# Cross-attention with head size 32: probabilities turned by VectorE's 32x32 squares and transfers instead of TensorE, value sums normalised after the product

## The chip, the cores and the metric

The kernel runs on one core of one Trainium2 chip. The metric is the device time of one execution in microseconds (us), median of several runs. Only the first attention of the network, about 230 us of some 2250 us, is touched.

## The reference

The network is a stack of two models over the same activations, x of 8 batches x 112 rows x 512, and the same context of 8 batches x 375 keys x 512. The changed part is the attention of the first model (16 heads of size 32):

```python
B, LQ, _ = hidden_states.shape          # 8, 112, 512
q = (x @ q_w + q_b).reshape(B, LQ, H, HD).transpose(0, 2, 1, 3)       # H = 16, HD = 32
k = (encoder_hidden_states @ k_w + k_b).reshape(B, LK, H, HD)...      # LK = 375
v = (encoder_hidden_states @ v_w + v_b).reshape(B, LK, H, HD)...
scores = jnp.einsum('bhqd,bhkd->bhqk', q, k) * scale
scores = jnp.where(mask, scores, mask_value)
attn = jax.nn.softmax(scores, axis=-1)
out = jnp.einsum('bhqk,bhkd->bhqd', attn, v)
out = out.transpose(0, 2, 1, 3).reshape(B, LQ, D) @ cproj_w + cproj_b
hidden = out + residual                 # then layer norm, fc, gelu, proj, residual
```

The second model follows: two cross-attentions with 16 heads of size 128, and an MLP. It is not changed.

## The kernel before

All is float32; a product of two float32 operands is three fp32r products over high and low halves (`product`, L1892 to L1894). Each engine runs its own hand-ordered program; semaphores join them. The changed stage is `attend_first`, which exists once for each engine. The stage before it writes the queries to memory, the stage behind it (`project` with layer 0) is the output projection and the next layer norm.

The stage runs over 8 batches, and in each over 4 tiles `t` of four heads, so over 32 tiles; a head of a tile is a unit `j`. In the iteration of tile T:

- TensorE (PE) makes the scores of the four heads of tile T+1 (`score_quad`, L2012: three rounds of four 32-row products into four banks `ps_s0`, of which one is the bank `ps_t[1]` and one `ps_o[1]`). Then for each j it turns the probabilities of head j of tile T with three transposes into one bank (`turn`, L2025), and fills in a quarter of other work (`fill`: half a key tile for tile T+2 by `key`, or part of the values of the next batch by `value`). At the end `weighted` (L2037) multiplies the turned probabilities by the values: 12 plain float32 products into `ps_o0`.
- ScalarE (ACT) evicts each turned head to `prob_t` in SBUF (`turned`, L1106), makes the exponentials of tile T+1 with their row sums (`exp`, L1110), the high half of the keys (L1100), the value tiles (L1086) and the high half of the output (`output_hi`, L1116).
- VectorE (DVE) makes the masked maxima of tile T+1 from the score banks (`masked_maximum`, L1576), and behind each exponential the reciprocal of the row sum (L1550) and the normalisation of the 112x375 probabilities (L1553), both in `normalize`; further the low half of the keys (L1559), of the output (`output_lo`, L1586) and of the queries (`split_q`, L1546), and once in a batch the high half of a context (`context_hi`, L1530).
- GpSimd (POOL) makes the low half of a context once in a batch (L916).
- SyncE (SP) issues all DMAs, on one queue. In this stage these are, once in a batch, the queries of the next batch (L687), a copy of the context from memory to memory for later (L636) and the context of the batch after the next (L632); further, in the first and the last batch, four transfers of weights (L612).

The second model's attention already has what the change brings to the first, once in a batch (not in a tile): VectorE turns 32x32 squares into an image `blocks` of 128 x 1536 (L1682), SP stores it (768 KB, `store_blocks`, L746), waits until it has landed, and loads it back with bands and squares exchanged, in four DMAs of 192 KB into 32 partitions each (`load_turned`, L756):

```python
src = turned_scr[place.parity].rearrange("(i a) (s f) -> s a i f", i=BANDS, s=4)
for s in range(4):
    rows = slice(SQUARE * s, SQUARE * (s + 1))
    dst = pt[place.parity][1][rows, :].bitcast(F32).rearrange("a (i f) -> a i f", i=BANDS)
    sp.dma_start(dst, src[s]).then_inc(turned_in[place.parity], 16)
```

Of the kernel before, what the change touches and what calls it, by code (L numbers as in the profile page):

```python
# [9 lines left out]
ALU = mybir.AluOpType  # L10
# [173 lines left out]

def wait(eng, sem, value):

    if isinstance(value, int) and value <= 0:
        return
    eng.wait_ge(sem, value)


def build(nc, x_in, ctx_in, kd_in_all, mask_in, blocks_a, blocks_b, vec_a, vec_b, value_rows, value_bias_rows, row_bias, eye, out):
# [7 lines left out]
    with ExitStack() as ctx:  # L200
# [15 lines left out]
        with ExitStack() as first_use:  # L216
# [5 lines left out]
            prob_2 = passing("prob2", [P, LK])  # L222
        sums_hi = sb("sums_hi", [P, DT, 4 * HALF], F32R)
        with ExitStack() as first_use:
            act_t_lo = passing("act_t_lo", [P, DT, ROWS], F32R)
            ctx_raw = [passing(f"ctx_raw{i}", [P, 3 * D]) for i in range(2)]
            prob_3 = passing("prob3", [P, LK])
        sums_lo = sb("sums_lo", [P, DT, 4 * HALF], F32R)
        act_t, sums = [act_t_hi, act_t_lo], [sums_hi, sums_lo]
        with ExitStack() as first_use:  # L230
            shared = passing("shared", [P, SUB0 * 3 * LQ])
            mask_u8 = passing("mask_u8", [LQ, NB * LK], U8)
            key_add = passing("key_add", [LQ, LK])
        extra = sb("extra", [P, 4 * NT * P + HALF])
# [15 lines left out]
        prob_t = [shared[:, 3 * LQ * i:3 * LQ * (i + 1)] for i in range(SUB0)]  # L250
# [5 lines left out]
        blocks = sb("blocks", [P, BLOCKS * P])  # L256
        extra_p = sb("extra_p", [P, 2 * NT])
# [20 lines left out]
        ps_s0, ps_t0, ps_o0 = [*ps_s, ps_t[1], ps_o[1]], ps_t[0], ps_o[0]  # L278
# [33 lines left out]
        t_mm, t_ev, av_mm = sem("t_mm"), sem("t_ev"), sem("av_mm")  # L312
# [83 lines left out]
        def turn_bank(place, t, j):  # L396

            return ps_v if place.final and t == 0 and j % 2 else ps_t0

# [4 lines left out]
        def key_evicted(place, t, j):  # L404

            if place.final:
                return place.key(t + 2) if j == 2 and t < 2 else None
            kind, part = fill(place, t, j)
            return part[0:2] if kind == KEY and part[2][1] == DT else None
# [193 lines left out]
        def _(sp):  # L603
# [277 lines left out]
        def _(pool):  # L881
# [44 lines left out]
            def attend_first():  # L926
                def one_batch(place):
                    for t in range(NT):
                        if t == 2 and place.after(2):
                            context_lo(place.after(2))  # L930

# [62 lines left out]
        def _(act):  # L994
# [98 lines left out]

            def attend_first():
# [8 lines left out]
                def turned(place, t, j):  # L1103
                    act.wait_ge(t_mm, place.unit + SUB0 * t + j + 1)
                    wait(act, av_mm, place.tile + t)
                    act.activation(prob_t[j][:], turn_bank(place, t, j)[:, 0:3 * LQ], ACT.Identity).then_inc(t_ev, 1)  # L1106

# [6 lines left out]
                def output_hi(place, t):  # L1114
                    act.wait_ge(av_mm, place.tile + t + 1)
                    act.activation(act_t[0][:, t, ds(place.b * LQ, LQ)], ps_o0[:, 0:LQ], ACT.Identity,  # L1116
                                   bias=col_a[:, C_BV0 + t:C_BV0 + t + 1]).then_inc(o_ev, 1)
# [15 lines left out]
                def tile(place, t):  # L1133
                    following = place.key(t + 1)
                    turned(place, t, 0)
                    if t == 2:
                        turned(place, t, 1)
                        exp(*following, 0)
                        value_finished(place, t, 0)
                        turned(place, t, 2)  # L1140
                        exp(*following, 1)
                        turned(place, t, 3)
                        key_hi(*place.key(t + 2))
                    else:
                        exp(*following, 0)
                        turned(place, t, 1)
                        exp(*following, 1)
# [1146 lines left out]
```

## Time and profile before

| | |
|---|---|
| median of 3 runs (lowest, highest) | 2255.64 us (2251.97, 2256.19) |
| the profiled execution | 2253.02 us |
| its span, first to last instruction | 2251.1 us |
| PE, DVE, ACT, POOL busy over the span | 98%, 62%, 54%, 40% |
| granted TensorE clock | 1.00 |

The profile is of one execution. A busy PE is not a PE at its peak, since a product's time on the page overlaps that of the next one; what a product costs is read from the distance of two starts. Windows of the trace are given in us from the span's start. The changed stage lies between about 54 us and 289 us.

### The profile page before, as it was taken

To read this page: it belongs to the slowest core of one execution; us is meant where nothing else is said; L and a number is where in the kernel's file an instruction comes from. 1 tells how busy PE (TensorE), PEld (TensorE's weight loads), DVE (VectorE), ACT (ScalarE), POOL (GpSimd) and SP (SyncE) were. 2 spreads that over 40 slices of the span, in tenths; PEclk is the share of its full clock that TensorE was granted. 3 is DMA by queue.
4 is the path that set the end of the run, shared out by engine and by line. 5 is a ranking of instruction groups with operands and counts; after the bars stand their busy time and mean duration, and the time that the engine had idled before them with its cause. 6 is when DMAs were issued, how large, how long until landed. Compare 5 with 4: busy or idle time off the path is not lost.

```text
span 2251.1 us, 36587 instructions
## 1 busy us (share of the span) xinstructions
PE 2210.7 (98%) x12347; PEld 2003.3 (89%) x12347; DVE 1387.8 (62%) x3070; ACT 1206.6 (54%) x2346; POOL 900.6 (40%) x1201
## 2 busy tenths in 40 slices
PE   7999999999999999999999999999999999999999
PEld 6777788889999999999988898999999999988888
DVE  6887784434766666666654526766666666655743
ACT  5777753345556555555554445555555565553421
POOL 2111045522545545544532233454554454432421
PEclk9999999999999999999999999999999999999999
DMA  5311126564768877877965456776977877774110
GB/s 184 116 65 65 53 76 205 184 214 154 253 208 251 256 232 236 265 234 220 282 209 154 160 181 197 252 234 206 281 240 222 260 243 229 235 226 132 47 50 33
DMA packets 316505, 424.61 MB, mean 189 GB/s; under 512 B 64670, under 2 KB 248882, under 8 KB 316194
## 3 DMA queue, kind: packets, MB, share of 16 engines
q1 hardware_dynamic: 316322, 422.28, 60.3%
q8 instruction: 102, 1.67, 0.3%
q14 instruction: 81, 0.66, 0.1%
HBM read 325.60 MB, written 102.76 MB: 190 GB/s over the span
## 4 chain that ended last, share of the span: by engine, by line
PE 85%; DVE 5%; DMA 4%; issue 3%; ACT 2%; POOL 1%; SPq 1%; DVEq 0%; ACTq 0%; POOLq 0%
PE ps_o L1892 7%; PE ps_o L1894 7%; PE ps_o L1893 7%; PE ps_v L1892 6%; PE ps_k L1892 6%; PE ps_k L1893 6%; PE ps_k L1894 6%; PE ps_v L1894 6%; PE ps_v L1893 6%; PE ps_t L1893 5%; PE ps_t L1894 5%; PE ps_t L1892 5%; PE ps_s L1892 4%; PE ps_s L1894 4%; PE ps_s L1893 4%
## 5 line engine op out<-in xcount | busy, mean ns | idle before, releaser
L924 POOL TENSOR_TENSOR cs_lo<-cs_lo,cs_hi 128x376 fp32r<-128x376 f32 x256 | 249.3, 1004 | 250.4 <-ACT cs_hi L1080 249.7
L947 POOL TENSOR_TENSOR pt_lo<-pt_lo,pt_hi 128x512 fp32r<-128x512 f32 x186 | 246.8, 1353 | 168.9 <-ACT pt_hi L1231 168.9
L1266 ACT ACTIVATE prob<-ps_s,row_columns 128x376 f32<-128x376 f32 x256 | 147.1, 575 | 192.7 <-DVE row_columns L1664 190.7
L888 POOL TENSOR_TENSOR w_b_lo<-w_raw_b,w_b_hi 128x512 fp32r<-128x512 f32 x80 | 110.0, 1395 | 323.4 <-ACT w_b_hi L1003 323.3
L1892 PE MATMUL ps_k<-cs_hi,w_a_hi 128*128 128x376 f32 x636 | 217.5, 342 | 0.0
L1664 DVE TENSOR_REDUCE row_columns<-ps_s 128x1 f32<-128x376 f32 x256 | 139.4, 545 | 123.2 <-PE ps_s L1894 122.6
L1893 PE MATMUL ps_k<-cs_lo,w_a_hi 128*128 128x376 f32 x636 | 213.0, 335 | 0.0
L1894 PE MATMUL ps_k<-cs_hi,w_a_lo 128*128 128x376 f32 x636 | 211.7, 333 | 0.0
L1553 DVE TENSOR_SCALAR prob<-prob,row_columns 128x375 f32<-128x375 f32 (+1 forms) x384 | 208.9, 544 | 4.5
L1682 DVE STREAM_TRANSPOSE blocks<-prob 128x384 f32<-128x384 f32 x240 | 138.8, 579 | 93.9 <-DMA turned_probabilities<-blocks 87.1
L1892 PE MATMUL ps_t<-cs_hi,w_a_hi 128*128 128x376 f32 x512 | 170.5, 333 | 1.4 <-DVE q L1546 1.4
L1893 PE MATMUL ps_t<-cs_lo,w_a_hi 128*128 128x376 f32 x512 | 170.7, 333 | 0.0
L1894 PE MATMUL ps_t<-cs_hi,w_a_lo 128*128 128x376 f32 x512 | 170.0, 332 | 0.0
L888 POOL TENSOR_TENSOR w_a_lo<-w_raw_a,w_a_hi 128x512 fp32r<-128x512 f32 x76 | 101.0, 1348 | 163.0 <-ACT w_a_hi L1003 163.0
L1892 PE MATMUL ps_v<-pt_hi,ckd 128*128 128x448 f32 (+1 forms) x384 | 144.0, 375 | 5.1 <-POOL pt_lo L947 4.3
L1244 ACT ACTIVATE sums_hi<-ps_v 128x448 fp32r<-128x448 f32 x128 | 69.7, 545 | 141.6 <-PE ps_v L1894 141.4
L1894 PE MATMUL ps_o<-pt_hi,ckd 128*128 128x448 f32 (+1 forms) x384 | 142.5, 371 | 0.0
L1894 PE MATMUL ps_v<-pt_hi,ckd 128*128 128x448 f32 (+1 forms) x384 | 142.4, 371 | 0.0
L1892 PE MATMUL ps_o<-pt_hi,ckd 128*128 128x448 f32 (+1 forms) x384 | 142.0, 370 | 0.1
L1893 PE MATMUL ps_v<-pt_lo,ckd 128*128 128x448 f32 (+1 forms) x384 | 141.8, 369 | 0.0
L1893 PE MATMUL ps_o<-pt_lo,ckd 128*128 128x448 f32 (+1 forms) x384 | 141.3, 368 | 0.0
L940 POOL CAST k_hi<-xk_hi 128x1 fp32r<-128x1 f32 x256 | 56.0, 219 | 207.0 <-PE ps_s L1894 206.6
(293 smaller groups left out, 6448.8 us busy)
## 6 DMA issues: line engine op xcount, KB each, us to landing
ckd<-context_by_key_halves SPq DMA_DIRECT2D x256, 384.0 KB, 5.1
cs_lo<-context SPq DMA_DIRECT2D x64, 752.0 KB, 6.7
pt_lo<-turned_probabilities SPq DMA_DIRECT2D x248, 192.0 KB, 3.8
turned_probabilities<-blocks SPq DMA_DIRECT2D x60, 768.0 KB, 4.4
w_raw_b<-in_blocks_b SPq DMA_DIRECT2D x104, 256.0 KB, 3.7
w_raw_a<-in_blocks_a SPq DMA_DIRECT2D x104, 256.0 KB, 5.1
q<-q_scratch SPq DMA_DIRECT2D x64, 256.0 KB, 3.5
extra<-extra_probability SPq DMA_DIRECT2D x32, 512.0 KB, 5.8
```

The source lines that it names most:

```text
L888: pool.tensor_tensor(w[slot][1][:, :, part], w_raw[slot][:, :, part], w[slot][0][:, :, part], ALU.subtract).then_inc(w_lo[slot], 1)
L924: pool.tensor_tensor(lo[:, part], lo[:, part].bitcast(F32), hi[:, part], ALU.subtract).then_inc(cs_lo, 1)
L940: pool.tensor_copy(k[t % 2][0][:, LK:KW], xk[0][:, ds(col, 1)])
L947: pool.tensor_tensor(lo, lo.bitcast(F32), hi, ALU.subtract).then_inc(t_lo, 1)
L1244: act.activation(sums[0][:, d, place.quarter * HALF:(place.quarter + 1) * HALF], ps_c[d % 2][:, 0:HALF], ACT.Identity).then_inc(c_hi, 1)
L1266: act.activation(prob[buf][:, 0:KW], ps_s[buf][:, 0:KW], ACT.Exp, bias=max_neg[:, buf:buf + 1], accum_out=prob_sum[:, buf:buf + 1]).then_i ...
L1553: dve.tensor_scalar(p[rows, 0:LK], p[rows, 0:LK], prob_rcp[rows, col:col + 1], None, ALU.mult).then_inc(s_norm, 1)
L1664: dve.tensor_reduce(max_neg[:, t % 2:t % 2 + 1], ps_s[t % 2][:, 0:KW], AX_X, ALU.max, negate=True).then_inc(s_max, 1)
L1682: dve.transpose(image(place).rearrange("p (s j t e) -> p t j s e", s=4, j=3, t=NT)[:, t], prob[buf][:, 0:BLOCKS * SQUARE].rearrange("p (j ...
L1892: pe.matmul(out, w_h, m_h, start=first, stop=False)
L1893: pe.matmul(out, w_h, m_l, start=False, stop=False)
L1894: return pe.matmul(out, w_l, m_h, start=False, stop=last)
```

## The change

- `turn` and `turned` go: no transposes of probabilities on PE, no evictions of them on ACT, no `prob_t`.
- Probabilities are not normalised. Behind each exponential VectorE transposes its 32x32 squares into an image of the tile (`squares_0`, 112x384, into one of two images). SP stores the image (768 KB) and, once it has landed, loads it back in four DMAs (`store_squares`, `load_squares`), once in each of the 32 tiles.
- `weighted` reads the loaded image, with 128 columns instead of 112, and runs one tile later: in the iteration of tile T it is that of tile T-1. The last tile's lies in `project`.
- The row sums' reciprocals are spread over 32 columns a head by one VectorE reciprocal of 112x128 a tile (`widened`), turned by one PE transpose (`reciprocals`), evicted by ACT (`rcp_out`) and multiplied onto the value sums (`normalized_0`), from which `output_hi` and `output_lo` now read.
- `context_hi` moves from DVE to ACT, `split_q` from DVE to POOL, `context_lo` one tile later. On SP, the query load, the copy and the context load are now placed between tiles' loads and stores.
- Four memsets of 128x384 stand ahead of the first maxima.

The core of the diff:

```diff
+images_0 = [shared[:], blocks[:]]
+rcp_rows = sb("rcp_rows", [P, P])
+o_rows = [sb(f"o_rows{i}", [P, LQ]) for i in range(2)]
...
 @block.sync
+                def store_squares(tile):
+                    sp.wait_ge(sq_turn, SUB0 * (tile + 1))
+                    wait(sp, sq_in[tile % 2], 64 * (tile // 2))
+                    sp.dma_start(turned_scr[tile % 2], images_0[tile % 2]).then_inc(sq_out, 16)
+
+                def load_squares(tile):
+                    sp.wait_ge(sq_out, 16 * (tile + 1))
+                    wait(sp, av_mm, tile - 1)
+                    src = turned_scr[tile % 2].rearrange("(i a) (s f) -> s a i f", i=BANDS, s=4)
+                    for s in range(4):
+                        rows = slice(SQUARE * s, SQUARE * (s + 1))
+                        dst = pt[tile % 2][1][rows, :].bitcast(F32).rearrange("a (i f) -> a i f", i=BANDS)
+                        sp.dma_start(dst, src[s]).then_inc(sq_in[tile % 2], 16)
 
                 def one_batch(place):
-                    if not place.final:
-                        load_q(place.next())
-                    copy_context(place.b)
-                    if place.after(2):
-                        load_context(place.after(2))
-                    if isinstance(place.b, int) and place.b == 0:
-                        load_block(1, 1)
-                    if place.swap:
-                        load_block(1, place.block_b + 2)
+                    for t in range(NT):
+                        load_squares(place.tile + t)
+                        if t == 0 and not place.final:
+                            load_q(place.next())
+                        if t == 1:
+                            copy_context(place.b)
+                        if t == 0 and place.after(2):
+                            load_context(place.after(2))
+                        if t == 2 and isinstance(place.b, int) and place.b == 0:
+                            load_block(1, 1)
+                        if t == 2 and place.swap:
+                            load_block(1, place.block_b + 2)
+                        if place.key(t + 1):
+                            store_squares(place.tile + t + 1)
...
 @block.scalar
-                def turned(place, t, j): ...
+                def rcp_out(place, t):
+                    act.wait_ge(rcp_mm, place.tile + t + 1)
+                    wait(act, o_lo, place.tile + t - 1)
+                    act.activation(o_rows[t % 2][:], rcp_bank(), ACT.Identity).then_inc(rcp_ev, 1)
...
 @block.vector
+            def normalized_0(place, t):
+                tile = place.tile + t
+                dve.wait_ge(av_mm, tile + 1)
+                dve.wait_ge(rcp_ev, tile + 1)
+                dve.tensor_tensor(o_rows[t % 2][:], ps_o0[:, 0:LQ], o_rows[t % 2][:], ALU.mult).then_inc(o_norm, 1)
...
-                def normalized_0(place, t, j):
-                    normalize(place.unit + SUB0 * t + j, prob_0[j], j)
+                def squares_0(place, t, j):
+                    tile = place.tile + t
+                    dve.wait_ge(s_exp, place.unit + SUB0 * t + j + 1)
+                    if j == 0:
+                        wait(dve, sq_out, 16 * (tile - 1))
+                    dve.transpose(images_0[tile % 2].rearrange("p (s j h e) -> p h j s e", s=4, j=3, h=SUB0)[:, j],
+                                  prob_0[j][:, 0:3 * P].rearrange("p (j s e) -> p j s e", j=3, s=4)).then_inc(sq_turn, 1)
+
+                def widened(place, t):
+                    tile = place.tile + t
+                    wait(dve, rcp_mm, tile)
+                    dve.reciprocal(rcp_rows[0:LQ, :].rearrange("p (h e) -> p h e", h=SUB0),
+                                   prob_sum[0:LQ, :].unsqueeze(2).broadcast_to([LQ, SUB0, HD0])).then_inc(rcp_wide, 1)
...
 @block.tensor
+            def weighted(place, t):
+                tile = place.tile + t
+                wait(pe, o_norm, tile)
+                pe.wait_ge(sq_in[tile % 2], 64 * (tile // 2 + 1))
+                ...  (12 products, moving turned_0(tile), 128 columns)
+                def reciprocals(place, t):
+                    tile = place.tile + t
+                    pe.wait_ge(rcp_wide, tile + 1)
+                    wait(pe, rcp_ev, tile)
+                    pe.transpose(rcp_bank(), rcp_rows[0:LQ, :], ident[0:LQ, 0:LQ]).then_inc(rcp_mm, 1)
-                def turn(place, t, j): ...
                         for j in range(SUB0):
-                            turn(place, t, j)
+                            if j == 2:
+                                reciprocals(place, t)
...
-                        weighted(place, t)
+                        if tile_before(place, t):
+                            weighted(*tile_before(place, t))
```

## Rows read from the trace of the kernel before

**Rows 1.** Busy time of each engine, batch by batch; granted clock, DMA share and GB/s last

```profile
core 0: us, PE busy (x) PEld busy (x) DVE busy (x) ACT busy (x) POOL busy (x), PEclk, DMA share, GB/s
...
143.40:171.90 28.50, 28.37 (x282) 22.66 (x280) 22.75 (x76) 21.97 (x61) 4.09 (x4) 1.00 0.20 64
...
257.40:289.30 31.90, 28.96 (x265) 22.96 (x258) 25.97 (x79) 22.68 (x60) 0.00 (x0) 1.00 0.36 117
```

**Rows 2.** The chain that ended last, in order of time: start, us, what

```profile
142.46 0.23 PE ps_v L1894
142.69 0.71 PE ps_o L2037 x24
...
145.44 0.17 PE ps_k L1894
145.61 0.30 PE ps_t L2025 x3
...
171.18 0.21 PE ps_o L2037
...
288.55 0.72 PE ps_o L2037 x24
289.26 1.04 PE ps_t L1902 x8
```

**Rows 3.** ACT's groups of instructions in one batch, 142.62 to 171.11 us

```profile
L1106 ACT ACTIVATE shared<-ps_t 128x336 f32<-128x336 f32 x16 | 7.2, 449 | 4.1 <-PE ps_t L2025 4.0
L1116 ACT ACTIVATE act_t_hi<-ps_o,col_a 128x112 fp32r<-128x112 f32 x4 | 1.4, 346 | 0.4 <-PE ps_o L2037 0.3
```

**Rows 4.** DVE's groups in the same batch

```profile
L1553 DVE TENSOR_SCALAR prob<-prob,row_columns 112x375 f32<-112x375 f32 x16 | 7.6, 473 | 0.6
L1550 DVE RECIPROCAL row_columns<-row_columns 112x1 f32<-112x1 f32 x16 | 2.6, 160 | 0.9 <-ACT prob L1110 0.9
L1586 DVE SCALAR_TENSOR_TENSOR act_t_lo<-ps_o,col_a,act_t_hi 128x112 fp32r<-128x112 f32 x4 | 1.3, 332 | 0.5 <-ACT act_t_hi L1116 0.3
L1530 DVE CAST cs_hi<-ctx_raw 128x1504 fp32r<-128x1504 f32 x1 | 0.9, 940 | 0.0
L1546 DVE TENSOR_TENSOR q<-q 128x448 fp32r<-128x448 f32 x1 | 0.6, 625 | 0.1
```

**Rows 5.** DVE's groups of the whole trace, for operations not yet in the stage

```profile
L1682 DVE STREAM_TRANSPOSE blocks<-prob 128x384 f32<-128x384 f32 x240 | 138.8, 579 | 93.9 <-DMA turned_probabilities<-blocks 87.1
...
L1754 DVE TENSOR_TENSOR q<-cs_hi,cs_lo 128x1344 fp32r<-128x1344 f32 x2 | 3.1, 1548 | 0.0
...
L1883 DVE MEMSET ps_t<- 128x512 f32 x2 | 1.0, 485 | 0.2
...
L1476 DVE TENSOR_TENSOR key_add<-prob 32x128 f32<-32x128 f32 x1 | 0.3, 274 | 0.0
```

**Rows 6.** One line's instructions: min/median/max ns, first and last start in us

```profile
L1231 ACT ACTIVATE pt_hi<-pt_lo x62: 1476/1479/1492, 563.5 to 1983.7; 128x1536 fp32r<-128x1536 f32 x62
```

**Rows 7.** SP's queue in the second model's attention: start, time to issue, transfer

```profile
604.75 0.32 SPq L746 DMA_DIRECT2D turned_probabilities<-blocks  x1
...
608.42 1.74 SPq L756 DMA_DIRECT2D pt_lo<-turned_probabilities  x4
...
626.30 1.74 SPq L756 DMA_DIRECT2D pt_lo<-turned_probabilities  x4
628.15 0.36 SPq L647 DMA_DIRECT2D ckd<-context_by_key_halves  x1
```

**Rows 8.** Issue to landing (last number, us) of the transfers issued at 604.75, 626.30, 628.15

```profile
turned_probabilities<-blocks SPq DMA_DIRECT2D x1, 768.0 KB, 3.6
...
pt_lo<-turned_probabilities SPq DMA_DIRECT2D x4, 192.0 KB, 3.6
...
ckd<-context_by_key_halves SPq DMA_DIRECT2D x1, 384.0 KB, 4.8
```

**Rows 9.** All 62 stores of such an image in the trace

```profile
DMA to landing us min/median/max: 3.3/4.4/6.8
```

**Rows 10.** DMA share and GB/s: queries, copy and context; a store; four loads

```profile
130.40:138.40 8.00, 7.86 (x75) 6.35 (x76) 7.50 (x22) 5.76 (x17) 4.08 (x4) 1.00 0.65 224
605.40:608.10 2.70, 2.70 (x17) 2.68 (x16) 1.78 (x5) 2.14 (x4) 0.00 (x0) 1.00 0.98 315
609.30:613.50 4.20, 4.20 (x25) 4.05 (x24) 3.19 (x8) 1.78 (x4) 3.70 (x8) 1.00 0.90 219
```

**Rows 11.** SP's queue in one batch of the changed stage

```profile
130.50 0.37 SPq L687 DMA_DIRECT2D q<-q_scratch  x1
130.92 0.51 SPq L636 DMA_DIRECT2D context<-in_ctx_t  x1
131.54 0.51 SPq L632 DMA_DIRECT2D ctx_raw<-in_ctx_t  x1
```

**Rows 12.** DVE at the start of the stage, in order of time

```profile
55.02 0.61 DVE L1559 SCALAR_TENSOR_TENSOR k_lo<-ps_o,col_a,k_hi 128x376 fp32r<-128x376 f32 x1 [0.85 <-ACT k_hi L1100]
...
60.62 0.42 DVE L1553 TENSOR_SCALAR prob<-prob,row_columns 112x375 f32<-112x375 f32 x1
```

More of the change, by code:

```diff
@@ L394, in fill, with tile_before, turned_0, rcp_bank @@
             return (None, None) if place.final else (VALUE, (place.next(), *part))
-        def turn_bank(place, t, j):
-            return ps_v if place.final and t == 0 and j % 2 else ps_t0
         def first_row_bank(r):
             return ps_o[1] if r == RT - 1 else (ps_v, ps_k)[r % 2]
[L404 to L409, printed above, removed]
+        def tile_before(place, t):
+            if t:
+                return place, t - 1
+            last = place.before()
+            return (last, NT - 1) if last else None
+        def turned_0(tile):
+            return pt[tile % 2][1][:].bitcast(F32).rearrange("p (i j h e) -> p j h i e", i=BANDS, j=3, h=SUB0)
+        def rcp_bank():
+            return ps_t[0][:, 0:LQ]
         def row_place(e, r):
@@ L928, in one_batch, with split_q_lo @@
                     for t in range(NT):
-                        if t == 2 and place.after(2):
+                        if t == 1 and not place.final:
+                            split_q_lo(place.next())
+                        if t == 3 and place.after(2):
                             context_lo(place.after(2))
+                def split_q_lo(place):
+                    pool.wait_ge(q_hi, place.batch + 1)
+                    hi, lo = q_by_layer[0][place.parity]
+                    pool.tensor_tensor(lo, lo.bitcast(F32), hi, ALU.subtract).then_inc(q_lo, 1)
                 batches_first(pool, skip, one_batch)
@@ L1609, in prologue @@
                         dve.wait_ge(q_out[i], 32)
+                    for t in prob_0:
+                        last = dve.memset(t[:, 0:3 * P], 0.0)
+                    last.then_inc(cleared, 1)
+                    dve.wait_ge(cleared, 3)
                     for j in range(SUB0):
@@ L1632, in one_batch @@
                                 add_y(0, 0, 0)
-                            if (t, j) == (2, 0) and place.after(2):
-                                wait(dve, k_mm, place.after(2).tile - NT)
-                                context_hi(place.after(2))
                         if place.final and t == 2:
@@ L2000, in first_row @@
                     last.then_inc(y_mm, 1)
-            def attend_first():
+            def weighted(place, t):
+                tile = place.tile + t
+                wait(pe, o_norm, tile)
+                if t == 0:
+                    pe.wait_ge(v_ev, 3 * place.batch + 3)
+                pe.wait_ge(sq_in[tile % 2], 64 * (tile // 2 + 1))
+                for i, n in enumerate(n for _, n in KEY_TILES):
+                    for j in range(SUB0):
+                        rows = slice(HD0 * j, HD0 * (j + 1))
+                        last = pe.matmul(ps_o0[rows, 0:P], v[place.parity][0:n, i, t * P + rows.start:t * P + rows.stop],
+                                         turned_0(tile)[0:n, i, j], start=(i == 0), stop=(i == 2))
+                last.then_inc(av_mm, 1)
+            def attend_first():
+                def reciprocals(place, t):
[3 more added lines that the diff above has]
+                    pe.transpose(rcp_bank(), rcp_rows[0:LQ, :], ident[0:LQ, 0:LQ]).then_inc(rcp_mm, 1)
                 def score_quad(place, t):
```

185 lines of the change are left out of this document (78 added, 107 removed).

## The prediction

> **What bounds the kernel now.** I read the table by stretches first, batch by batch. A batch of the changed stage takes 28.5 us: the value product of its last tile starts at 142.69, that of the next batch at 171.18 [rows 2]. PE is busy 28.37 of 28.50 us; DVE 22.75, ACT 21.97, and the DMA engines stand at a share of 0.20 [rows 1]. The other full batches have the same numbers. Then I read the chain of waits: it runs from product to product on PE, and a turn of one head stands in it with 0.30 us between two key products 0.17 us apart [rows 2]. So the stage is bound by PE, at the granted clock 1.00, which is 2.4 GHz. Last I read how long a transfer of each kind takes, in the stage that already stores and reloads such an image [rows 7 to 10]. The reader is to see two things: PE has something to give, and the DMA engines, idle here today, are about to get a load that one row at a time looks harmless and in a loop is not.
>
> **PE.** 16 turns a batch at 0.30 us go: 4.8 us. The first turn of a tile costs some 0.15 us more, 0.6 us a batch. Added: four transposes of the reciprocals, at most the price of a turn, 1.2 us; 128 columns instead of 112 in four value products of 0.71 us [rows 2], 4 x 0.71 x 16/112 = 0.4 us. PE's work in a batch becomes about 28.5 - 5.4 + 1.6 = 24.7 us.
>
> **ACT.** 16 evictions at 449 ns go [rows 3]; consecutive instructions overlap by about 0.1 us, so 16 x 0.35 = 5.6 us. Added: four evictions of 128x112, like those at 346 ns [rows 3], 1.0 us without the overlap, and the context's high half, 128x1504, by its like of 128x1536 at 1479 ns [rows 6], 1.5 us. 22.0 - 5.6 + 2.5 = 18.9 us a batch: not the bound.
>
> **DVE.** Out go 16 normalisations at 473 ns and 16 reciprocals at 160 ns [rows 4], less overlap 16 x 0.52 = 8.3 us; the cast of the context and the subtraction of the queries, 0.94 + 0.62 less overlap, 1.4 us [rows 4]. In come 16 transposes like those at 579 ns [rows 5], 16 x 0.5 = 8.0 us; four products of 128x112 like those at 332 ns [rows 4], 1.0 us; and four reciprocals of 112x128. The trace has reciprocals of one column only, 160 ns. Below, a wide one costs as much as another operation on 128 columns, 274 ns [rows 5]; above, I take a row with some ten times as many elements, 1548 ns for 1344 [rows 5]. Less the overlap that is 0.2 to 1.4 us each, 0.8 to 5.6 us a batch. DVE's work becomes 22.75 - 8.3 - 1.4 + 8.0 + 1.0 = 22.0, and with the reciprocals 22.9 to 27.7 us. I take the low end: of the two rows the 128-column one is the nearer. Neither end passes 28.5.
>
> The Trainium skill ("VectorE: DVE Perf Modes", First, the fixed hardware budget) says that the reciprocal iterates its divide "with a repeat count of 8". An estimate by it, eight steps for each of 128 columns, is 1024 steps, near the upper end; the one-column row can't tell the two apart.
>
> **POOL.** The queries' low half is one more subtraction a batch beside four; POOL is busy 4.1 of 28.5 us [rows 1], so this is hidden.
>
> So by the engines alone a batch would fall to about 25 us. What remains is SP and the transfers.
>
> **SP's loop.** SP runs, for each tile T: wait until the store of T has landed, issue its four loads, issue the batch's extras, wait for the squares of T+1, issue the store of T+1, and again wait for its landing. One queue, in order. `weighted` of each tile needs its loads, so no tile can take less than this loop. Its parts:
> - Four loads take 1.74 us to issue, and what stands behind them is issued 1.85 us after the first (626.30 to 628.15) [rows 7].
> - A store with nothing much ahead of it lands 3.6 us after its issue [rows 8]. If that held here, the loop would be 1.85 + 3.6 = 5.5 us a tile, and it would fit.
> - But here each store is issued right behind the loads of the tile before. The trace shows what becomes of a transfer in that place: the 384 KB transfer issued at 628.15 lands 4.8 us later [rows 8], so 1.85 + 4.8 = 6.65 us after the first load's issue. The loads themselves end late: the last is issued some 1.3 us behind the first and lands 3.6 us later [rows 8], and in 609.30 to 613.50 the engines are at a share of 0.90 while they move only 219 GB/s, against 315 GB/s at 0.98 for a store [rows 10].
> - The store has 768 KB, twice as much. The second half, 393 kB at 315 GB/s [rows 10], is 1.25 us: 7.9 us. If all of it were hidden, 6.65 us. I take 7.5 us, nearer to the upper end, since the engines have no share left to hide it in.
>
> The squares are not late for it: DVE's work is 5.7 to 6.9 us a tile and PE's 6.2, and the loop comes back only after 7.5 us. What sets the pace is store, landing, loads, store, not the arithmetic.
>
> The Trainium skill ("SBUF — State Buffer", Door 1: The DMA port swizzle) says that 32 partitions reach 8 of 16 ports, half the rate of 128. The trace agrees: 219 GB/s in the window of the loads into 32 partitions each, against 315 GB/s. With loads at the store's rate the loop would be about a microsecond shorter, 6.5 us, and the verdict below the same.
>
> **The extras.** Queries, copy and context now stand between loads and store, so the store queues behind them too. Together they occupy 0.65 x 8.00 = 5.2 us of the sixteen engines [rows 10, 11]. Before, this lay beside PE's work with the engines otherwise idle; now it is added to the loop.
>
> A batch is then 4 x 7.5 + 5.2 = 35.2 us against 28.5. The loop pays only below (28.5 - 5.2) / 4 = 5.8 us a tile.
>
> **The sum.** Start of the stage: four memsets of 384 columns, by the 485 ns of 512 [rows 5] some 0.35 us each, stand between the last key work at 55.02 and the maxima and delay the first tile's probabilities, ready at 61.0 [rows 12], by 1.4 us; the first store is issued near 62 and the first load 3.6 us later, at 65.6. From there 31 loops to the last tile's loads: 31 x 7.5 = 232.5 us. Extras: I split the 5.2 us as 0.9 for the queries and 2.15 each for copy and context; 7 query loads, 8 copies, 6 contexts give 36.4 us. Eight weight transfers of 256 KB, 2.1 MB at 315 GB/s, 6.7 us. The last loads are issued at 65.6 + 232.5 + 43.1 = 341.2 and landed 5 us later, 346. Before, the last value product starts at 288.55 [rows 2]. That is 57.6 us later. Some of what follows it before (a row of the projection, 12 products of 0.23 = 2.8 us, two turned rows, 1.04 us [rows 2], and DVE's share) is now done ahead of it: 5 us back. Net +53 us. On the profiled execution, 2253.0, this gives 2306; the median of the runs shown is 2.6 us above that execution, so 2308 us.
>
> **The rivals.**
> - *The transfers hide (ends faster).* The place is the store behind the loads. If the engines took its packets while the loads wait for SBUF, it would land after 3.6 us whatever is ahead, and the loop is 5.5 us. With the extras in the loop a batch is 4 x 5.45 + 5.2 = 27.0 us, and seven batches and the longer start give 2246; with the extras hidden too, PE and DVE decide with about 25 us, and it is 3.5 x 7.5 - 1.4 = 25 us faster, 2228. It decides below 5.8 us a tile. For it: the shares of 0.90 leave a little room. Against it: the 4.8 us of a transfer of half the size in just that place.
> - *The reciprocal takes DVE.* With 1.4 us a tile, DVE's work is 27.7 us a batch and its waits for exponentials come on top: no gain, 2250 to 2256. It shows only if the loop is short, so its chance lies inside those of faster and same.
> - *The loop is longer than I think.* Pile-up of copy and context, and landings that drift from the 3.6 us towards the median of 4.4 or the longest of 6.8 [rows 9]: 8.5 us a tile, 31 us more, 2339.
> - *The clock.* PE would wait a quarter of each tile. Rows show 1.00 throughout, also in the last batch, where PE is busy 28.96 of 31.90 us [rows 1]. If it fell to the lower level, 1.2 GHz, in these waits, PE's 6.2 us a tile would be up to 12.4 and the stage far above 2345. I have no row for it.
>
> **How the numbers follow.** My forecast, a loop between 6.8 and 8.6 us, 2275 to 2345: 0.72. The loop a little shorter, 2260 to 2275: 0.04. Beyond 2345, by pile-up or clock: 0.05. Together slower 0.81. Within 0.2%, which is about 4.5 us and as little as a measurement of this kernel can tell: 0.05, the point where the loop is near 5.8 us or the reciprocal eats the gain. Faster 0.14: 0.08 near 2246, 0.06 near 2228. The range 2252 to 2345 leaves out the faster cases and the worst, 0.19. The likeliest case alone: 2275 to 2345.
>
> **What would show it.** In the profile after, PE in the stage busy for about 25 of 35 us a batch and waiting at `weighted` for the transfers into `pt_lo`; DMA share near 0.9 and some 230 GB/s in place of 64; four loads every 7.5 us in SP's queue, farther apart in the first two tiles of a batch; landing of the stores 5 to 6 us instead of 3.6; the last value product near 346 us. The wide reciprocal's row gives its price. I am wrong if the stores behind loads land in under 4 us, or if PE's last wait is for VectorE.

## The result, and the profile after

The changed kernel takes 2337.09 us (median of 5 runs, 2333.44 to 2337.49), the kernel before 2255.64 (median of 5). The ratio is 1.0361, 95% interval 1.0347 to 1.0375: 3.6% slower. The profiled execution spans 2335.3 us. Forecast were 2308 us, in a range of 2252 to 2345.

First the busy time of the engines in two batches of the stage, the ones that answer to [rows 1].

```profile
core 0: us, PE busy (x) PEld busy (x) DVE busy (x) ACT busy (x) POOL busy (x), PEclk, DMA share, GB/s
...
145.03:183.41 38.38, 28.51 (x245) 22.82 (x248) 25.27 (x67) 18.39 (x49) 5.01 (x5) 0.87 0.73 211
257.40:295.93 38.53, 29.10 (x273) 22.93 (x272) 25.88 (x69) 19.45 (x53) 5.08 (x5) 0.91 0.73 218
```

A batch takes 38.4 us instead of 28.5. No engine is full: PE 28.5, DVE 25.3, ACT 18.4. The DMA engines went from a share of 0.20 to 0.73 at 211 GB/s; forecast were a share near 0.9 and some 230 GB/s. They are not busy all the time even in a tile without other transfers: in the one that starts at 137.50 their share is 0.07 in the first 1.0 us, about 1.0 at 292 GB/s in the next 5.1 us (138.50 to 143.60), and 0.13 in the last 1.4. PE's 28.5 us are not the work it had before: the granted clock is 0.87, and part of that busy time runs at the lower level, 1.2 GHz.

SP's queue shows the loop (start, time to issue, transfer, number):

```profile
130.03 1.73 SPq L721 DMA_DIRECT2D pt_lo<-turned_probabilities  x4
...
137.50 1.73 SPq L721 DMA_DIRECT2D pt_lo<-turned_probabilities  x4
139.36 0.35 SPq L711 DMA_DIRECT2D turned_probabilities<-shared  x1
145.03 1.73 SPq L721 DMA_DIRECT2D pt_lo<-turned_probabilities  x4
146.80 0.43 SPq L698 DMA_DIRECT2D q<-q_scratch  x1
147.35 0.43 SPq L643 DMA_DIRECT2D ctx_raw<-in_ctx_t  x1
147.91 1.45 SPq L711 DMA_DIRECT2D turned_probabilities<-blocks  x1
156.23 1.74 SPq L721 DMA_DIRECT2D pt_lo<-turned_probabilities  x4
158.01 0.52 SPq L647 DMA_DIRECT2D context<-in_ctx_t  x1
158.66 0.50 SPq L711 DMA_DIRECT2D turned_probabilities<-shared  x1
168.25 1.73 SPq L721 DMA_DIRECT2D pt_lo<-turned_probabilities  x4
```

Read it from group of loads to group of loads. With loads and store alone a tile takes 7.5 us (130.03, 137.50, 145.03). With the queries and a context between them it takes 11.2 (to 156.23), with a copy 12.0 (to 168.25). Issue to landing, in the stretches of the stores at 139.36, 147.91 and 158.66:

```profile
turned_probabilities<-shared SPq DMA_DIRECT2D x1, 768.0 KB, 5.6
...
turned_probabilities<-blocks SPq DMA_DIRECT2D x1, 768.0 KB, 8.2
...
turned_probabilities<-shared SPq DMA_DIRECT2D x1, 768.0 KB, 9.5
context<-in_ctx_t SPq DMA_DIRECT2D x1, 752.0 KB, 7.0
```

The chain of waits in 130 to 169 us (start, us, what) has the stores in it, 45% of the stretch by its sum over lines:

```profile
131.32 4.26 DMA pt_lo<-turned_probabilities
135.72 1.50 PE ps_o L2064 x24
...
139.06 0.31 PE ps_k L1944
...
145.25 0.80 PE ps_o L2064 x24
...
147.91 8.23 DMA turned_probabilities<-blocks
...
158.66 9.50 DMA turned_probabilities<-shared
```

The waits between 62 and 360 us (SP) and between 65.6 and 360.9 us (PE) say the same (us in total, times, longest). L710 is SP's wait for the squares ahead of a store; it waits for them once, in the first tile. (Two further waits of L716, 10.0 us, are put down to a product of PE, but in every tile the loads are issued within 0.15 us of the store's landing.)

```profile
SPq L716 <- DMA turned_probabilities<-shared: 98.2, 15, 9.1
SPq L716 <- DMA turned_probabilities<-blocks: 88.5, 14, 8.2
SPq L710 <- DVE shared L1623: 7.1, 1, 7.1
PE ps_o L2064 <- DMA pt_lo<-turned_probabilities: 71.1, 22, 6.2
```

In [rows 2] the chain was PE from end to end. The chain after also shows the clock: the 24 value products take 1.50 us at 135.72 and 0.80 at 145.25, and key products 0.17 us apart before are 0.31 apart at 139.

### The profile page after: what moved, and what is told of

Same layout as the page of the kernel before. It is cut to its first block, busy times and chain, and to the rows that moved or that the text cites. A ratio compares the mean times of both kernels' runs of the same rounds, so it can differ in the third digit from the quotient of the medians.

```text
span 2335.3 us, 35823 instructions
## 1 busy us (share of the span) xinstructions
PE 2216.7 (95%) x11995; PEld 2004.8 (86%) x11995; DVE 1408.2 (60%) x2997; ACT 1174.7 (50%) x2256; POOL 911.0 (39%) x1208
## 4 chain that ended last, share of the span: by engine, by line
PE 77%; DMA 12%; DVE 3%; SPq 3%; issue 2%; ACT 1%; POOL 1%; ACTq 0%; DVEq 0%; POOLq 0%
PE ps_o L1943 7%; PE ps_o L1945 7%; PE ps_o L1944 7%; DMA turned_probabilities<-blocks 5%; PE ps_k L1943 5%; PE ps_k L1944 5%; PE ps_k L1945 5%; PE ps_v L1943 5%; PE ps_v L1945 5%; PE ps_v L1944 5%; PE ps_t L1944 4%; PE ps_t L1945 4%; PE ps_t L1943 4%; DMA turned_probabilities<-shared 4%; PE ps_s L1943 4%; PE ps_s L1945 4%
## 5 line engine op out<-in xcount | busy, mean ns | idle before, releaser
L1943 PE MATMUL ps_k<-cs_hi,w_a_hi 128*128 128x376 f32 x636 | 223.6, 352 | 0.0
L1944 PE MATMUL ps_k<-cs_lo,w_a_hi 128*128 128x376 f32 x636 | 220.1, 346 | 0.0
L1945 PE MATMUL ps_k<-cs_hi,w_a_lo 128*128 128x376 f32 x636 | 217.4, 342 | 0.0
L1590 DVE TENSOR_SCALAR prob<-prob,row_columns 128x375 f32<-128x375 f32 x256 | 150.6, 588 | 0.1
```

What stands on the lines that cost most here:

```text
L1590: dve.tensor_scalar(p[rows, 0:LK], p[rows, 0:LK], prob_rcp[rows, col:col + 1], None, ALU.mult).then_inc(s_norm, 1)
L1943: pe.matmul(out, w_h, m_h, start=first, stop=False)
L1944: pe.matmul(out, w_h, m_l, start=False, stop=False)
L1945: return pe.matmul(out, w_l, m_h, start=False, stop=last)
```

## The experiments

The numbers are those of the order in which they ran; they stand here by the question that they answer.

Each ratio is to the kernel before, timed beside the run on the same chip. Its median there was 2260.6 to 2261.9 us for the first eleven runs and 2255.1 for the last, so the expectations, written on a scale of 2256, are compared by ratio; 2337 is 1.036.

**1. Loads over 128 partitions.** Is it the 32 partitions of each load that make the loop long?

```diff
-  src = turned_scr[tile % 2].rearrange("(i a) (s f) -> s a i f", i=BANDS, s=4)
+  src = turned_scr[tile % 2].rearrange("p (s f) -> s p f", s=4)
   for s in range(4):
-      rows = slice(SQUARE * s, SQUARE * (s + 1))
-      dst = pt[tile % 2][1][rows, :].bitcast(F32).rearrange("a (i f) -> a i f", i=BANDS)
+      dst = pt[tile % 2][1][:, 3 * P * s:3 * P * (s + 1)].bitcast(F32)
```

> Left out: the exchange of bands and squares between partitions; each of the four loads of a tile takes 128 partitions of 1536 bytes instead of 32 partitions of four pieces of 1536 bytes, so the number of loads, the piece and the bytes stay. If the partitions of the loads set their rate (219 GB/s against 315 GB/s of the store in the trace of the kernel before), the 768 KB of loads take 2.5 us instead of 3.6, the store queued behind them lands some 1.1 us sooner, a plain tile falls from 7.5 to about 6.4 us and 32 tiles give about 35 us: about 2300 us. If the partitions are not what holds them (piece size or a memory-to-chip limit), nothing moves: 2337 us, plain tile still 7.5.

Measured: 1.0351 (1.0323 to 1.0378), no different from the change. SP's queue, and the loads' median landing over 120 to 345 us (3.5 in the changed kernel):

```profile
133.97 1.75 SPq L720 DMA_DIRECT2D pt_lo<-turned_probabilities  x4
...
141.87 1.74 SPq L720 DMA_DIRECT2D pt_lo<-turned_probabilities  x4
...
149.26 2.44 SPq L720 DMA_DIRECT2D pt_lo<-turned_probabilities  x4
```
```profile
pt_lo<-turned_probabilities SPq DMA_DIRECT2D x99, 192.0 KB, 2.9
```

The median load lands after 2.9 us instead of 3.5, but plain tiles (those without extras) still take 7.9 and 7.4 us; the 14 of them have a mean of 7.46, against 7.45 in the changed kernel. The median hides which loads gained. In the plain tiles at 133.97, 141.87 and 173.41 the first load lands after 2.3 or 2.4 us (2.8 or 2.9 in the changed kernel's at 130.03, 137.50 and 168.25), but the last of the four after 4.6, 4.1 and 4.0 us, where it took 4.3, 4.4 and 4.2. The store behind them lands after 5.4 us, 5.5 before (medians of the 14 tiles). So loads over 128 partitions did not make a faster group of four, and buy the loop nothing. What a loop with a faster group would take, this run does not show.

**2. One straight hop, four transfers.**

```diff
-  sp.dma_start(turned_scr[tile % 2], images_0[tile % 2]).then_inc(sq_out, 16)
-  ...
+  part = slice(3 * P * s, 3 * P * (s + 1))
+  sp.dma_start(pt[tile % 2][1][:, part].bitcast(F32), images_0[tile % 2][:, part]).then_inc(sq_in[tile % 2], 16)
```

> Left out: the exchange of bands and squares between partitions, and with it the way through device memory: four transfers of 128 partitions go straight from the squares to the landed tile, so there is no store and no wait for its landing. If the loop of loads issued (1.85 us) plus store landed (5.6 us) sets the stage, it is gone: a batch falls from some 38 us to what PE and VectorE want (24.7 us of PE work predicted, 24.9 to 25.3 us of VectorE busy measured in the changed kernel), some 26 to 28 us, and the time to 2337 - 8 x 11 = about 2250 us, with the granted clock back at 1.00 in the stage. If PE, VectorE or the clock set the stage by themselves and the transfers only sit beside them, the batch stays above 34 us and the time above 2300 us.

Measured: 0.9963 (0.9951 to 0.9976). One batch of it:

```profile
125.04:150.51 25.47, 23.94 (x236) 19.08 (x232) 23.31 (x66) 17.83 (x49) 4.99 (x5) 1.00 0.55 194
```

25.5 us a batch, the clock at 1.00, PE busy 23.9: take the store and the wait for its landing away, and the arithmetic of the change is 3 us a batch faster than before, as its working said (24.7 of PE). So the whole loss lies in the way through device memory. The run takes away two things at once, the 768 KB of each store and the round trip of issue and landing; no run parts them. The gain of seven batches would be 21 us, and only 8 arrive. The last value product starts at 282.13, only 6.4 us before that of [rows 2], so most of the rest goes in the last batch, where PE stands 4.25 us for a low half of the projection's weights (see runs 5 and 10).

**3. Copies after the stage.**

```diff
-  if t == 1:
-      copy_context(place.b)
   ...
   batches_first(sp, prologue, one_batch)
+  for b in range(NB):
+      copy_context(b)
```

> The eight copies of the context within device memory (752 KB read and 752 KB written each) are issued after the stage instead of one in each batch. In the changed kernel a loop with such a copy took 12.0 us where a plain one took 7.5. If the copy costs the loop its own transfer time on the shared queue, the stage is shorter by 8 x 4.5 = 36 us and the time is about 2301 us, unless the eight copies, now in one heap before the loads of the next stage, hand back up to 8 x 4.5 us there. If the 12.0 us came from something else in that loop, the time stays at 2337 us.

Measured: 1.0238 (1.0220 to 1.0256), so 0.0123 x 2256 = 28 us less. All tiles without queries or weights are now plain; a copy in the loop had cost 3.8 us, eight of them 30.

**4. Extras on ScalarE's queue.**

```diff
-  sp.dma_start(dst, src).then_inc(q_in[place.parity], 16)
+  act.dma_start(dst, src).then_inc(q_in[place.parity], 16)
   (the context and the copy likewise)
```

> The queries, the context and the copy of each batch are issued from ScalarE's queue instead of SyncE's; bytes stay. If they cost the loop because the store of the next tile stands behind them in one first-in first-out queue, the loop with them falls from 11.2 to 12.0 us to about 8.5 us, 8 x (3 + 3.5) = 50 us: about 2287 us. If they cost it because the sixteen engines of the DMA are shared whatever the queue, the store is slowed as much by sharing: 2325 to 2337 us.

Measured: 1.0283 (1.0267 to 1.0298), 18 us less: between the two. Another queue lets the store past the extras in part, but not past their use of the sixteen engines: issued 1.5 us behind a context on ScalarE's queue, the store at 131.67 lands after 8.7 us, where the one at 152.15, without extras, lands after 5.7. The run also changes when the extras are issued, since they now stand in ScalarE's program.

**8. The store ahead of the extras.** The same queue and the same bytes; only the place of one line:

```diff
   load_squares(place.tile + t)
+  if place.key(t + 1):
+      store_squares(place.tile + t + 1)
   if t == 0 and not place.final:
       load_q(place.next())
   ...
-  if place.key(t + 1):
-      store_squares(place.tile + t + 1)
```

> The changed kernel with the store of the next tile issued right behind the loads of this one, ahead of the queries, the context, the copy and the weights; bytes and count stay. If the extras cost the loop because the store stands behind their data in the queue, the store lands in 5.6 us again, the extras move behind it and are carried in part in the 1.7 us a loop in which nothing is in flight: up to 1.7 us for each of about 20 loops with extras, 2303 to 2320. If the loop pays for bytes and not for order, the next loads wait for the extras in place of the store: 2332 to 2337.

Measured: 1.0147 (1.0132 to 1.0162), 48 us less than the change, and more than the 34 us that order was given at its best. SP's queue with the queries and a context, and with a copy, and the stage by engines:

```profile
130.58 2.14 SPq L721 DMA_DIRECT2D pt_lo<-turned_probabilities  x4
132.85 0.35 SPq L711 DMA_DIRECT2D turned_probabilities<-blocks  x1
133.25 0.43 SPq L698 DMA_DIRECT2D q<-q_scratch  x1
133.79 1.24 SPq L643 DMA_DIRECT2D ctx_raw<-in_ctx_t  x1
138.99 1.74 SPq L721 DMA_DIRECT2D pt_lo<-turned_probabilities  x4
140.85 0.35 SPq L711 DMA_DIRECT2D turned_probabilities<-shared  x1
141.25 0.52 SPq L647 DMA_DIRECT2D context<-in_ctx_t  x1
146.97 2.81 SPq L721 DMA_DIRECT2D pt_lo<-turned_probabilities  x4
```
```profile
98.75:130.58 31.83, 25.28 (x232) 20.05 (x231) 23.91 (x65) 18.01 (x49) 5.01 (x5) 0.95 0.81 255
```

The tiles with extras take 8.4 and 8.0 us instead of 11.2 and 12.0 (means of the stage: 7.8 and 8.1 instead of 11.7 and 11.2). The DMA engines are at 0.81 and 255 GB/s instead of 0.73 and 211: the extras run while SP waits for a landing and issues again, when otherwise almost nothing is in flight (the shares of 0.07 and 0.13 above). From the first group of loads to the last, 65.34 to 310.26, it is 244.9 us; in the changed kernel, 65.60 to 360.90, it is 295.3.

**7. A narrow reciprocal in the changed kernel.**

```diff
-  dve.reciprocal(rcp_rows..., prob_sum[0:LQ, :].unsqueeze(2).broadcast_to([LQ, SUB0, HD0]))
+  dve.reciprocal(rcp_four[0:LQ, :], prob_sum[0:LQ, :])
+  dve.tensor_copy(rcp_rows..., rcp_four[0:LQ, :].unsqueeze(2).broadcast_to([LQ, SUB0, HD0]))
```

> The changed kernel with the reciprocal taken of the four sums and then copied out to 128 columns, instead of a reciprocal of 128 columns (0.91 us each). VectorE is spared some 0.5 us a tile. If SyncE's loop sets the stage, nothing moves: 2337, within 3 us. If VectorE (24.9 to 25.3 us busy of 35 to 38 in a batch) held it in places, up to 32 x 0.5 = 16 us less: about 2321.

Measured: 1.0355 (1.0334 to 1.0377), nothing. The price of the wide one in the changed kernel, then the two instructions of this run:

```profile
L1630 DVE RECIPROCAL rcp_rows<-row_columns 112x128 f32<-112x128 f32 x21 | 19.1, 910 | 0.0
```
```profile
L1634 DVE COPY rcp_rows<-rcp_four 112x128 f32<-112x128 f32 x32 | 7.3, 227 | 1.1
L1631 DVE RECIPROCAL rcp_four<-row_columns 112x4 f32<-112x4 f32 x32 | 4.3, 134 | 0.0
```

DVE is off the path here.

**6. The normalisation behind the product, alone,** on the kernel before.

```diff
-  pe.wait_ge(s_norm, unit + 1)
+  pe.wait_ge(s_exp, unit + 1)
   (turns of unnormalised probabilities; o_rows = ps_o0 * reciprocals behind the product)
```

> One part alone on the kernel before: TensorE still turns the probabilities, unnormalised, and the value sums are normalised behind the product (wide reciprocal, its turn on TensorE, one product a tile on VectorE). VectorE loses 16 x (0.47 + 0.16) = 10.1 us a batch and gains 4 x (0.91 + 0.26) = 4.7. If the kernel before is bound by PE in the stage (28.4 of 28.5 us busy), this buys nothing and costs the added turns: 4 x 0.1 us a batch, about +3 us, 2256 to 2262. If part of what the change was to give came from taking the probabilities' normalisation off the way to PE, the batch falls below 28 us and the time below 2250.

Measured: 1.0031 (1.0020 to 1.0041), some 7 us slower. Two value products a batch apart in its chain, and a stretch of 28.5 us:

```profile
152.13 0.71 PE ps_o L2080 x24
...
181.18 0.72 PE ps_o L2080 x24
```
```profile
145.00:173.50 28.50, 28.27 (x272) 22.94 (x272) 17.92 (x51) 21.73 (x63) 3.86 (x4) 1.00 0.19 64
```

A batch takes 29.05 us instead of 28.5. DVE has lost 4.8 us (22.75 to 17.92) and nobody was waiting for it; PE has four turns more. This half of the change buys nothing by itself.

**5. The whole exchange in one hop.** Sixteen transfers a tile, eight from SP and eight from POOL:

```diff
+  dst = pt[tile % 2][1][SQUARE * s:SQUARE * (s + 1), 3 * P * i:3 * P * (i + 1)].bitcast(F32)
+  src = images_0[tile % 2][SQUARE * i:SQUARE * (i + 1), 3 * P * s:3 * P * (s + 1)]
+  eng.dma_start(dst, src)          # bands 0, 1: SP; bands 2, 3: POOL
```

> The whole exchange in one hop: sixteen transfers of 32 partitions x 1536 bytes a tile straight from the squares to their landed places, eight issued by SyncE and eight by GpSimd; no device memory in between, nothing left out. In the run of four straight transfers a tile SyncE took 0.60 us for each issue, so eight take some 4.8 us, under the 6.4 us of a tile there. If GpSimd issues at a like rate, the batch stays near 25.5 us and the time near that run's, 0.3 to 0.5% below the kernel before (about 2250 on the scale of 2256). If GpSimd needs more than 0.9 us for each, its eight set the tile: at 1.2 us each 9.6 us a tile, 32 x (9.6 - 6.4) = 100 us more, about 2350.

Measured: 1.0020 (1.0009 to 1.0032). GpSimd issues one in 0.50 us, so it doesn't set the tile, and six batches take 26.8 us each (88.90 to 249.42 in SP's queue), 1.7 less than before. Yet the whole is no faster. Where it goes is in the last batch: what PE does there (in brackets the wait before it, and for whom), and the granted clock around it:

```profile
262.09 0.79 PE L1945 MATMUL ps_v<-w_b_hi,act_t_hi 128*128 128x512 f32 x1 [4.25 <-DVE w_b_lo L1445]
262.68 0.63 PE L1946 MATMUL ps_v<-w_b_lo,act_t_hi 128*128 128x512 f32 x1
263.11 0.63 PE L1947 MATMUL ps_v<-w_b_hi,act_t_lo 128*128 128x512 f32 x1
...
269.27 0.39 PE L1946 MATMUL ps_k<-w_b_lo,act_t_hi 128*128 128x512 f32 x1
269.50 0.40 PE L1947 MATMUL ps_k<-w_b_hi,act_t_lo 128*128 128x512 f32 x1
```
```profile
260.00:270.00 10.00, 7.91 (x53) 5.73 (x54) 6.01 (x18) 3.83 (x11) 0.90 (x3) 0.66 0.35 110
270.00:286.00 16.00, 13.30 (x79) 9.93 (x81) 13.39 (x33) 7.03 (x18) 7.05 (x15) 0.89 0.75 217
286.00:300.00 14.00, 10.28 (x86) 7.98 (x79) 9.94 (x24) 6.73 (x20) 0.00 (x0) 0.81 0.40 126
```

PE stands 4.3 us for a low half of the projection's weights, then works at 1.2 GHz: products 0.43 us apart instead of 0.23. In the kernel before, the same stretch has gaps of 0.7, 1.1 and 0.7 us with turns between them, and a clock of 1.00. The last value product starts at 290.47, 1.9 us behind that of [rows 2], though six batches had gained 10 us: the last batch loses them. The first store of the next stage (`context_by_key_halves`) is issued at 334.21 instead of 330.80, 3.4 us late, so another 1.5 us go behind that product. Run 2 has the same wait of 4.25 us for `w_b_lo` in its last batch.

**9 and 10. The one hop, with the narrow reciprocal, and with a reordered last batch as well.** In run 10 ScalarE splits all four parts of the projection's weights in the first tile of the last batch, and the halves of the keys come a step sooner:

```diff
-  if t < 2:
-      projection_part(place, 2 * t)
+  if t == 0:
+      projection_part(place, 0)
   ... (parts 1, 2 and 3 also at t == 0, behind exp 1, 2 and 3)
```

> The one-hop kernel (sixteen transfers a tile, nothing left out) with the reciprocal taken of four columns and copied out (0.13 + 0.23 us in place of 0.91 us a tile). In the changed kernel this moved nothing, because SyncE's loop was ahead of VectorE; with one hop VectorE is busy 32.8 to 34.0 us of 38 to 39 and PE waits for its low halves of the keys and its maxima. If VectorE is the bound now, the batch falls by up to 4 x 0.55 = 2.2 us from 27 us, 8 x 2.2 = 17 us: about 2247 on the scale of 2256. If PE or the issue of the transfers is, it stays at 1.002 of the kernel before.

> As the run with the narrow reciprocal, and in the last batch ScalarE splits all four parts of the projection's weights in its first tile and both engines take the halves of the keys one step sooner. In the one-hop run PE stood still for 4.3 and 2.7 us in the last batch, waiting for low halves of weights and for sums, and the granted clock after it was 0.84 and 0.92 over 70 us. If the tail is where the one hop's gain went, the stall of 4.3 us and up to 0.1 x 70 = 7 us of slow clock come back: 5 to 11 us below the run with the narrow reciprocal. If the clock would have fallen anyway, only the 4 us come back or less.

Measured: 1.0014 (1.0005 to 1.0023) and 1.0000 (0.9991 to 1.0009). The reciprocal bought next to nothing here too; six batches take 26.7 and 26.6 us each, so its time is not what holds them. The waits of PE in six batches point elsewhere, though no run tests it: in run 5 PE waits 7.0 us for the low half of the keys (`k_lo`, VectorE), in runs 9 and 10 5.4 and 5.5, in run 2 not at all; and VectorE waits 8.9, 9.1 and 9.6 us for transfers to leave the image that it is to overwrite, in run 2 again not at all. The six batches of run 5 are 7.0 us longer than those of run 2. The last batch's order moved the next stage's first store from 332.19 to 327.81 us, 4.4 us, of which about 3 are seen at the end. The clock still falls, to 0.72 in 250 to 260 us, where PE is busy for 6.7 us of 10.

**12. GpSimd's other work moved round its issues.**

```diff
-  if t == 1 and not place.final:
+  if t == 2 and not place.final:
       split_q_lo(place.next())
   if t == 3 and place.after(2):
-      context_lo(place.after(2))
+      context_lo(place.after(2), range(2))
+  if t == 0 and place.batch and not place.final:
+      context_lo(place.next(), range(2, DT))
```

> The one-hop kernel with its narrow reciprocal and its last batch's order, and with GpSimd's other work moved round its eight issues a tile: the low half of the queries behind the issues of the third tile instead of ahead of them (GpSimd stood 4.2 us there waiting for ScalarE), the low halves of the context in two pieces of two in place of one of four (3.8 us). The run with four straight transfers a tile, none of them on GpSimd, had batches of 25.5 us where the one-hop runs have 26.5 to 27.5. If it is GpSimd's order that costs the difference, the batch falls to about 25.5 and 7 x 1.0 to 1.5 = 7 to 10 us come off a ratio of 1.000: 0.996 to 0.997 of the kernel before. If it is SyncE's eight issues of 0.62 us (5.0 us a tile) or VectorE, it stays within 0.998 to 1.001.

Measured: 1.0140 (1.0121 to 1.0158): a miss, and a bad one. I had counted only the key products as users of the context's low half. The value products of the next batch start in the first tile, too, and wait for all four pieces. SP's loads, then POOL's pieces and PE's wait in the same tile:

```profile
118.06 4.95 SPq L423 DMA_DIRECT2D pt_lo<-shared  x8
...
130.04 5.23 SPq L423 DMA_DIRECT2D pt_lo<-blocks  x7
```
```profile
122.54 1.92 POOL L945 TENSOR_TENSOR cs_lo<-ctx_raw,cs_hi 128x376 fp32r<-128x376 f32 x2
```
```profile
124.56 0.47 PE L1954 MATMUL ps_v<-w_b_hi,cs_hi 128*128 128x512 f32 x1 [4.65 <-issue]
```

The first tile of a batch takes 12.0 us. GpSimd's last two pieces end at 124.5, and PE's value product, idle for 4.65 us, starts at 124.56. The profile names no releaser there; in another batch it names `cs_lo` for 5.4 us. So the run says nothing about the rest of POOL's order: that stays open.

**11. Store first, copies after the stage, narrow reciprocal, reordered last batch,** still through device memory.

> The run with the store ahead of the extras, with the copies after the stage, the narrow reciprocal and the last batch's reordering as well; nothing left out. The way through device memory stays, so its floor is a plain loop of 7.5 us: 32 x 7.5 = 240 us from the first load at 65 us, 5 us sooner than in the run before it (245 us): 2280 to 2290, still above the kernel before. If VectorE or the copies had held the loop at 7.5 to 8.0 us, the loop falls below 7.3 us and the time below 2275.

Measured: 1.0123 (1.0108 to 1.0138). From 66.05 to 299.07 us the loads of 30 further tiles take 233.0 us, 7.8 each, with the copies gone from among them. Even if all extras were free, a tile would have to come under 28.5 / 4 = 7.1 us to pay. The way through device memory, in the orders tried, does not get there.

## Why the prediction held, and where it was off

- **The mechanism.** "What remains is SP and the transfers": right. The first store came at 62.26 (near 62 forecast), the first load at 65.60 (65.6 forecast). A plain tile was put at 7.5 us; 14 such tiles of the stage have a mean of 7.45, and the store behind the loads lands after some 5.6 us. Run 2 shows that the way through device memory is at fault and nothing else. The exact hit is partly luck: 7.5 was chosen between 6.65 and 7.9 because the DMA engines were taken to have no share left, and they stand for some 2 us of each plain tile.
- **The extras: the term that was mis-sized.** They were put at 5.2 us a batch, their time on the sixteen engines at the share that they had when nobody waited for them. In the loop the queries with a context cost 4.2 us a batch (3.05 forecast), a copy 3.8 (2.15), eight weight transfers 7.7 in all (6.7). With 1.0 us for the one tile that has queries alone, that is 6 x 4.2 + 1.0 + 8 x 3.8 + 7.7 = 64 us where the sum had 43. (These are the tiles' means less 7.45, so they add up to the measured 295 us of 31 tiles by themselves; they show where the time lies and are no check of it.) What the working didn't see is that this was a term of order, not of bytes: run 8 moves one line and gets back 48 us, more than all that the sum had set down for them. They cost 64 us ahead of the store and 14 behind it (244.9 less 31 x 7.45).
- **The end.** 5 us were to come back behind the last value product, by work done ahead. That product starts at 366.61, 78.1 us later than before (57.6 forecast), and the next stage's first store at 410.02, 79.2 us later: not 5 back but 1 more. This is the second term that was mis-sized. The clock has a part in it: between the two, after PE has stood for 2.1 us, 12 products come 0.43 us apart instead of 0.23, which is 2.4 us more; the granted clock is 0.73 in 361 to 380 us, where the kernel before had 1.00. The span is 84.2 us longer (2335.3 against 2251.1); the last 5 us come up in stages that the change does not touch, and executions of the kernel before differ by more (2251.17 to 2258.25). So both misses pointed the same way, and the forecast was 29 us short of the median.
- **The clock: a rival without a row.** It did fall, to 0.87 in the stage, and cost next to nothing there: PE's busy time grew to 28.5 us a batch, 7.1 a tile (23.9 a batch in run 2), which is still under the loop's 7.5, and SP waited for no squares behind the first tile. The rival's time, "far above 2345", was that of PE at the lower level all the time, 12.4 us a tile; it was there only part of the time.
- **PE, ACT, DVE.** 24.7, 18.9 and 22.9 to 27.7 us a batch were forecast. Run 2, where nothing slows them, has 23.9, 17.8 and 23.3. I took the low end for the wide reciprocal; it is 0.91 us, between the bounds of 0.27 and 1.55. The Trainium skill ("VectorE: DVE Perf Modes", First, the fixed hardware budget) spoke for the upper end; 910 ns against 227 for a copy of the same 128 columns bears out that a reciprocal costs several times another operation; as whole instructions it is four times, not eight. It changed no time (run 7).
- **The partitions.** The rule of the Trainium skill ("SBUF — State Buffer", Door 1: The DMA port swizzle) was said to agree with the trace, and loads at the store's rate to give a loop of 6.5 us. Run 1 takes the 32 partitions away: the median load lands 0.6 us sooner, the last of the four does not, and the loop stays. So the partitions are not what keeps the loop from 6.5 us; whether loads at the store's rate would is untested. No number of the forecast hung on it.

"The transfers hide" fell: stores behind loads land after 5.6 us, not 3.6. Not tested is what holds the one-hop batches at 26.7 us where four transfers a tile give 25.6 (87.47 to 241.01, six batches); the waits under runs 9 and 10 point to VectorE's wait for the transfers out of the image. Open is also where run 10's 3.0 us at the next stage's first store (327.81 against 330.80) are gone at the end; the kernel before itself ranges from 2257.8 to 2264.9 beside it.

## What to carry to other kernels

When work moves from an engine to transfers, write down the loop that one in-order queue must go round (issue, landing, issue) and put everything else that this queue carries into it, in its place: ahead of the transfer that is waited for it costs its whole time, right behind it most of it is free (64 us against 14 here). Ask that question of the order before that of the bytes; here one line moved was worth 48 us. An engine that sheds work may also shed what bridged its gaps: check each wait that the removed work used to cover, in the last round above all.

## What the runs showed of the hardware that I had not expected

- The granted clock of TensorE was at the lower level behind stalls of a few us: in run 5, behind 4.3 us of standing still, products came 0.43 us apart, and 0.23 us apart again at 269.3. Two batches of the changed stage had 0.87 and 0.91, one of the straight hop (run 2) 1.00.
- Two transfers on two queues are not independent: beside a context on ScalarE's queue a store took 8.7 us to land instead of 5.7. With the extras on that queue the kernel got back 18 us, with the store ahead of them on the same queue 48.
- GpSimd issues a transfer of 48 KB in 0.50 us and SyncE in 0.62 us (32 partitions of SBUF to 32 of SBUF), and they land after 2.6 us (median; 1.8 to 5.8) in run 5; four of 192 KB in run 2 took SyncE 0.60 us each to issue.
- A wide reciprocal of 112x128 takes 910 ns (the changed kernel); of four columns, 134 ns (run 7).
